# Earlier first routing, a norm between the index writes, and gated sums on GpSimd in a decoder layer

## The reference

```python
x = x + attn(_layernorm(x), ...)              # L0_attn
x = x + xattn(_layernorm(x), ctx_1024, ...)   # L0_xattn: softmax(Q K^T / sqrt(8)) V, then @ Wo + bo
x = x + ffn(_layernorm(x), ...)               # L0_ffn:

scores = jnp.einsum('bsd,de->bse', x, Wr) + br
_, topk_idx = jax.lax.top_k(scores, K)                        # K = 2 of E = 8
indicator = jax.nn.one_hot(topk_idx, E).sum(-2)
weights = jax.nn.softmax(jnp.where(indicator > 0, scores, neg_inf), axis=-1)
for i in range(E):
    xi = x * indicator[..., i:i + 1]
    h = jax.nn.relu(jnp.einsum('bsd,dh->bsh', xi, W1[i]) + b1[i])     # 128 -> 512
    yi = jnp.einsum('bsh,hd->bsd', h, W2[i]) + b2[i]                  # 512 -> 128
    out = out + yi * weights[..., i:i + 1]
```

## Time and profile before

| what | value |
|---|---|
| median of three runs | 336.9 us |
| profiled execution | 336.61 us |
| its span, first to last instruction | 334.9 us |
| mean granted TensorE clock | 0.949 |
| busy: PE, DVE, ACT, POOL | 279.0, 197.3, 184.1, 136.4 us |

### The profile page before, as it was taken

The page is one execution under the profiler, slowest core; times in us unless marked ns, Lnnn a source line. Parts: engine busy times, 40 slices in busy tenths (PEclk is TensorE's granted clock), DMA queues, the critical chain, the costliest instruction groups (busy, mean ns, idle before and its releaser), DMA issues.

```text
span 334.9 us, 5929 instructions
## 1 busy us (share of the span) xinstructions
PE 279.0 (83%) x2035; PEld 206.1 (62%) x2035; DVE 197.3 (59%) x471; ACT 184.1 (55%) x513; POOL 136.4 (41%) x188
## 2 busy tenths in 40 slices
PE   5799999999989898978996886804539989988984
PEld 2677777877866675645553343402229989988973
DVE  3768564556297866774674752521453675565564
ACT  1779767378556663654576687503314555544431
POOL 7990460317032004310387854274381346544000
PEclk9999999999999999999998999775957999999999
DMA  8800035511950100010592700010062634500302
GB/s 241 192 1 3 4 46 66 64 15 41 229 116 0 48 2 3 3 33 17 152 251 54 231 0 5 1 40 24 18 178 78 230 116 138 187 18 11 96 0 64
DMA packets 27291, 25.24 MB, mean 75 GB/s; under 512 B 3866, under 2 KB 20332, under 8 KB 27260
## 3 DMA queue, kind: packets, MB, share of 16 engines
q1 hardware_dynamic: 24462, 22.46, 25.7%
q0 software_dynamic: 1216, 1.61, 1.6%
q10 hardware_dynamic: 1584, 0.80, 0.9%
HBM read 12.49 MB, written 4.80 MB: 52 GB/s over the span
## 4 chain that ended last, share of the span: by engine, by line
PE 57%; DVE 18%; issue 9%; DMA 5%; POOL 5%; ACT 3%; SPq 3%; POOLq 0%; ACTq 0%; DVEq 0%
PE ps L873 6%; PE ps L799 5%; PE ps L800 5%; PE ps L801 5%; PE ps L906 5%; PE ps L918 4%; PE ps L951 4%; DVE mneg L1534 3%; PE ps L988 3%; PE ps L1135 3%; POOL xs L685 3%; PE ps L880 2%; SPq L478 2%; PE ps L1137 2%; DVE hid_lo L1705 2%
## 5 line engine op out<-in xcount | busy, mean ns | idle before, releaser
L1254 ACT ACTIVATE p<-ps,negmax 128x256 f32<-128x256 f32 (+1 forms) x128 | 52.7, 426 | 25.2 <-DVE negmax L1505 24.9
L1534 DVE TENSOR_REDUCE mneg<-ps 128x2 f32<-128x512 f32 x64 | 42.5, 684 | 19.7 <-PE ps L951 19.6
L1284 ACT ACTIVATE px<-ps 128x512 f32<-128x512 f32 x64 | 36.2, 599 | 19.1 <-PE ps L973 18.8
L1505 DVE TENSOR_REDUCE negmax<-ps 128x2 f32<-128x512 f32 (+1 forms) x48 | 32.9, 686 | 19.6 <-PE ps L875 12.4
L1705 DVE SCALAR_TENSOR_TENSOR hid_lo<-ps,hid_hi 128x512 fp32r<-128x512 f32 x42 | 28.6, 689 | 25.7 <-ACT hid_hi L1327 25.6
L1327 ACT ACTIVATE hid_hi<-ps 128x512 fp32r<-128x512 f32 x42 | 25.1, 598 | 33.7 <-PE ps L801 33.6
L692 POOL DMA_INDIRECT ys<-yrow,xr x26 | 25.4, 976 | 27.5 <-DVE yrow L1711 21.3
L951 PE MATMUL ps<-k_st,q_mem 128*128 128x256 bf16 x128 | 24.8, 278 | 10.1 <-DVE mneg L1534 7.6
L596 POOL TENSOR_SCALAR tmp<-mv 128x2 f32<-128x2 f32 x8 | 1.8, 230 | 68.7 <-DVE mv L1529 68.5
L1240 ACT CAST t_hi<-ps 128x512 fp32r<-128x512 f32 x32 | 18.8, 592 | 19.5 <-PE ps L801 18.5
L1254 ACT ACTIVATION_READ_ACCUMULATOR p<-ps,negmax 128x1 f32 x128 | 26.6, 208 | 0.0
(11 more groups left out here) (268 smaller groups left out, 761.1 us busy)
## 6 DMA issues: line engine op xcount, KB each, us to landing
ovw<-w_hi SPq DMA_DIRECT2D x10, 256.0 KB, 3.0
ovw<-w_lo SPq DMA_DIRECT2D x10, 256.0 KB, 3.1
w_raw<-in_L_ffn_W SPq DMA_DIRECT2D x2, 1024.0 KB, 8.1
xs<-pad SPq DMA_DIRECT2D x1, 1716.0 KB, 10.3
k_st<-k_part SPq DMA_DIRECT2D x12, 128.0 KB
q_mem<-q_part SPq DMA_DIRECT2D x48, 32.0 KB
w_last<-in_L_ffn_W SPq DMA_DIRECT2D x4, 256.0 KB, 7.3
w_late<-in_L_ffn_W SPq DMA_DIRECT2D x4, 256.0 KB, 5.2
```

The costliest lines, as they stand in the source:

```text
L1254: last = act.activation(dst, bank[:, n * i:n * i + n], ACT.Exp, bias=negmax[:, kt, h:h + 1], accum_out=psums[:, kt, h:h + 1])
L1284: act.activation(px[:, (g // 2) % 2, c0:c0 + 512], ps[:, score_banks[k], :], ACT.Exp, scale=SCALE_X).then_inc(s_px, 1)
L1505: dve.tensor_reduce(dst, ps[:, k % 3, :].rearrange("p (h q) -> p h q", h=n), AX, ALU.max, negate=True).then_inc(s_max, 1)
L1534: dve.tensor_reduce(mneg[:, qt, :].rearrange("p (r g) -> p r g", r=2)[:, :, g], ps[:, max_bank[("MX", b, u)], :].rearrange("p (h k) -> p h ...
```

## The change

Four things are changed. First, the last output product of batch 2, the router's product of group 0 and `oq0` of batch 2 stand in a slot of their own in front of the first scores of batch 3, `NT` 0 in the last slot of batch 2, and `PS` 0 in the first slot of batch 3; the rest of batch 2's output comes half a slot to a slot earlier. Second, six small VectorE instructions that prepare the places of group 1 leave `places` and become a unit `PX` behind batch 2's residual. Third, GpSimd issues three of the eight writes of group 0, then `norm_3(2)`, then the other five and those of group 1; two low parts of the second weights move behind all writes. Fourth, the gated sums leave VectorE: GpSimd does them behind its last collect, each as a product and a sum.

```diff
+FIRST_OUT = 3
...
-            for g, unit in zip(((0, 0, 1, 2, 3, 5.5, 6.5), (1.5, 2.5, 3, 4.5, 5.5), (0.5, 1.5, 2, 3, 3.5), (0.5, 1, 1.5, 2, 2.5))[b], units):
+            for g, unit in zip(((0, 0, 1, 2, 3, 5.5, 6.5), (1.5, 2.5, 3, 4.5, 5.5), (0.5, 1.5, 2, 3, 3.5), (-1, 0, 0.5, 1.5, 2))[b], units):
...
-                    (2, 7): [("W2", 0, 1)], (3, -0.5): [("NT", 0)], (3, 0): [("RT", 0), ("XC", 1)],
-                    (3, 1): [("W2", 0, 2)], (3, 2): [("PS", 0)], (3, 3): [("W2", 0, 3)], (3, 4): [("NT", 1)],
-                    (3, 5): [("RT", 1), ("XC", 2)], (3, 6): [("W2", 0, 4)], (3, 6.5): [("PS", 1)]}
+                    (2, 7): [("W2", 0, 1), ("NT", 0)], (3, 0): [("XC", 1), ("PS", 0)], (3, 1): [("W2", 0, 2)],
+                    (3, 2): [("PX", 0)], (3, 3): [("W2", 0, 3)], (3, 4): [("NT", 1)], (3, 5): [("RT", 1), ("XC", 2)],
+                    (3, 6): [("W2", 0, 4)], (3, 6.5): [("PS", 1)]}
+            if b == last:
+
+                slots.append([("CO", b - 1, 3), ("RT", 0), ("oq0", b - 1)])
...
-                if g == 0 and b >= 1:
+                if g == 0 and 1 <= b < last:
                     slot += [("CO", b - 1, 3)]
...
-                  (4, 1, "h"): [("GT", 0)], (5, 1, "h"): [("WT", 0), ("GS", 1)],
-                  (NS + 6, 0, "h"): [("CB", 0)], (NS + 6, 1, "h"): [("CB", 1)], (NS + 7, 0, "h"): [("CB", 2)]}
+                  (4, 1, "h"): [("GT", 0)], (5, 1, "h"): [("WT", 0), ("GS", 1)]}
...
+            def add_pairs(b):
+                pool.wait_ge(s_yg[b], 16)
+                pool.wait_ge(s_gate, b // 2 + 1)
+                pool.wait_ge(s_n3, TPB * (b + 1))
+                for c in range(2):
+                    for t in range(TPB * b, TPB * b + TPB):
+                        row = yg[:, 2 * t + c, :]
+                        step(pool.tensor_scalar(row, row, gate[:, 2 + c, t:t + 1], None, ALU.mult))
+                        pool.tensor_tensor(resid[:, t, :], row, resid[:, t, :], ALU.add).then_inc(s_sum, 1)
+                    pool.wait_ge(s_sum, 2 * TPB * b + TPB * (c + 1))
...
-            for i in range(4):
-                second_weights(i)
+            second_weights(0)
+            second_weights(1)
             pool.wait_ge(s_init, 16)
-            for t in range(ROUTED[0][1]):
-                for c in range(2):
-                    dispatch(t, c)
+            early = [(t, c) for t in range(*ROUTED[0]) for c in range(2)]
+            for t, c in early[:FIRST_OUT]:
+                dispatch(t, c)
             norm_3(2)
+            for t, c in early[FIRST_OUT:]:
+                dispatch(t, c)
             for t in range(*ROUTED[1]):
                 for c in range(2):
                     dispatch(t, c)
+            second_weights(2)
+            second_weights(3)
             second_weights(4)
...
             for j in range(NS):
                 collect(j)
+            for b in range(B - 1):
+                add_pairs(b)
...
-                if g == 0:
-
-                    step(dve.tensor_tensor(base[:, :], now, delta, ALU.mult))
...
+            def carry():
+
+                now, delta = over[:, 0, :], shift[:, 0, :]
+                step(dve.tensor_tensor(base[:, :], now, delta, ALU.mult))
...
-            def add_pairs(b):
-                dve.wait_ge(s_yg[b], 16)
-                dve.wait_ge(s_n3, TPB * (b + 1))
-                for c in range(2):
-                    for t in range(TPB * b, TPB * b + TPB):
-                        dve.scalar_tensor_tensor(resid[:, t, :], yg[:, 2 * t + c, :], gate[:, 2 + c, t:t + 1],
-                                                 resid[:, t, :], ALU.mult, ALU.add).then_inc(s_sum, 1)
-                    dve.wait_ge(s_sum, 2 * TPB * b + TPB * (c + 1))
...
+                    elif kind == "PX":
+                        carry()
```

More of the change, by code:

```diff
@@ L265, in decoder_layer @@
         s_ovw = [sem(f"s_ovw{i}") for i in range(2)]
-        s_b2T, s_yev = sem("s_b2T"), sem("s_yev")
+        s_b2T, s_yev, s_gate = sem("s_b2T"), sem("s_yev"), sem("s_gate")
         s_rank, s_rank_ev = sem("s_rank"), sem("s_rank_ev")
@@ L1604, in two_gates @@
                 step(dve.tensor_tensor(gate[:, 3, ts], gate[:, 1, ts], gate[:, 2, ts], ALU.mult))
+                dve.sem_inc(s_gate, 1)
             def gates():
@@ L1658, in places @@
                                   ALU.add).then_inc(s_pos, 1)
-                if g == 0:
-                    step(dve.tensor_tensor(base[:, :], now, delta, ALU.mult))
-                    step(dve.tensor_tensor(base[:, :], base[:, :], tile0[:, :], ALU.add))
-                    step(dve.tensor_scalar(edge[:, :], now, float(CAP), float(CAP), ALU.mult, ALU.add))
-                    step(dve.tensor_reduce(taken[:, :], now, AX, ALU.add))
-                    step(dve.tensor_scalar(start[:, :], taken[:, :], float(CAP), float(CAP * NE), ALU.mult, ALU.add))
-                    step(dve.tensor_tensor(full[:, :], start[:, :].to_broadcast([P, NE]), edge[:, :], ALU.subtract))
+            def carry():
+                now, delta = over[:, 0, :], shift[:, 0, :]
+                step(dve.tensor_tensor(base[:, :], now, delta, ALU.mult))
+                step(dve.tensor_tensor(base[:, :], base[:, :], tile0[:, :], ALU.add))
+                step(dve.tensor_scalar(edge[:, :], now, float(CAP), float(CAP), ALU.mult, ALU.add))
+                step(dve.tensor_reduce(taken[:, :], now, AX, ALU.add))
+                step(dve.tensor_scalar(start[:, :], taken[:, :], float(CAP), float(CAP * NE), ALU.mult, ALU.add))
+                step(dve.tensor_tensor(full[:, :], start[:, :].to_broadcast([P, NE]), edge[:, :], ALU.subtract))
             def spares():
@@ L1775, in _ @@
                         finish_rows()
-                    elif kind == "CB":
-                        add_pairs(b)
 _INS = ['x', 'ctx_1024', 'L0_attn_W_qkv', 'L0_attn_b_qkv', 'L0_attn_W_o', 'L0_attn_b_o',
```

## The result

The changed kernel takes 325.22 us, the median of four runs (323.1 to 325.4; two more, at 322.95 and 325.57, leave it where it is), against 336.97 in the same session (336.76 to 337.2). The ratio is 0.963, with a 95% interval of 0.959 to 0.968. The forecast was 325.4. Its mechanism is the one that the trace shows, though several terms had the wrong size, and these made up for each other.

What follows compares the result with a forecast made beforehand. Bound: from 216 to 250 us, group 0's places and batch 2's norm with what follows, TensorE waiting 13.6 us. Gain 11.0 + 0.8 - 0.9 + 0.8 - 0.2 = 11.5 (9.7 to 14.0), giving 325.4; range 323.0 to 329.0.

Steps and rivals of the forecast that it cites:

- Places of group 0: Routing passage: with the last `CO` of batch 2 moved ahead, these places end at 211.95 instead of 216.73, 4.8 us earlier.
- The norm of batch 2: On GpSimd, bound by VectorE's statistics: starts at 217.3 instead of 228.29, gain 11.0 us (10.6 to 11.8).
- From the norm to the places of group 1: Chain behind batch 2's norm, 8.18 us before: gains 0.8 from more full clock, between nothing and 1.5.
- The collision of `spares`: Before the first `x_lo`: VectorE's two-input additions wait for GpSimd's moved low parts, costing 0.9 us (0 to 1.6).
- starved entirely: Worst case for `spares`: VectorE's additions get nothing through beside GpSimd's low parts, costing 1.6 us.
- The end: Last `hid_lo` on VectorE: gains 0.8 us without the gated sums, which GpSimd hides by nearly 5 us.
- The 0.2 set aside: Experts' end: 0.2 us lost if one `x_lo` with two SBUF inputs meets GpSimd's sum instructions.
- the slower rival: At the end, GpSimd's sums finish last: at 1.30 us an instruction the time is 338.2; chance 0.04.
- The late statistics: Batch 2's statistics come no earlier than 220.16, so the norm starts at 220.3 and the time is 328.4; chance 0.12.
- Wider collisions: VectorE instructions with one SBUF input also wait beside GpSimd: 3.0 us worse, 328.4 to 329; chance 0.08.
- That the norm gains only what the places gain: Something else orders batch 2's norm, so only 4.8 + 0.6 is left: 331.5 us; chance 0.06.
- Two signs of being wrong: TensorE waits elsewhere over 3 us between 216 and 236, or first `x_lo` to the end changes by over 1.5 us.

Runs made afterwards that it cites:

- the repeat: The changed kernel run once more with no edit, in the first set of experiments; 323.8 us, ratio 0.961.

## Why the prediction was right

**Places of group 0.** They end at 210.83, 5.9 earlier than before, or 4.66 without the 1.24; the forecast was 4.8. Moving `CO`, `RT` and the counting did what the prediction says (with the 1.24 added, `oT0` comes at 208.40 against 208.35), and the kernel with the slots alone shows that it pays only because GpSimd is free then.

**The norm of batch 2.** The bound is the one named, statistics behind `wo`, and three writes end 1.4 before it. The size was off: 10.2 instead of 11.0, below my lower end of 10.6. The forecast laid the statistics between 216.5 and 217.5 and chose 217.3. Without the 1.24 they are at 218.0. The cause is TensorE's clock: it was 0.50 for the whole stretch from 206 to 216, so that the `CO` took 1.94 where I reckoned with at most 1.67, and `wo` 1.22 instead of 1.06. The kernel with `wo` ahead of that `CO` starts the norm 1.3 earlier, as the rows ask. There, and in an execution that was granted more clock (the one with the sums on VectorE), the third write is the bound: its end and the norm's start are 0.1 apart. That the first write came 0.86 behind the places, not 0.28, cost nothing in the profiled execution, since its cover is those 1.4.

**From the norm to the places of group 1.** Here the sum was mis-sized: "I take 0.8", at most 1.5, and it is 1.9. The mechanism, a TensorE that comes out of work and not out of 13.6 us of waiting, was right. I counted only `CO`, `NT` and `RT`, 1.5 in all, and took half of it. All of TensorE's instructions of the chain are slower at half clock, the four scores between them too: of the 1.9, `CO` gives 0.85, `NT` and `RT` 0.44 and the scores 0.6 to 0.7 (differences of start times). The executions in which TensorE waits 7 to 14 us for the norm have 8.1 to 8.4 here, those with a wait of 2 us or less 6.3, and 6.77 where there is none.

**The collision of `spares`.** -0.9 forecast, -0.9 found, and 0.9 won back when the low parts moved. How it came about was not as worked out. I let each of VectorE's additions wait for one low part, three of them by the end. In truth the first addition met the second of the four low parts and was held until the fourth had ended, 3.04 us, and the others ran freely at 0.20. That is the case that I had called starved entirely and priced at 1.6. It cost 0.9, because `spares` has 11 instructions in the trace and not 12, and the low parts ended 10.0 behind the places and not 10.2. So the size agrees by luck. The Trainium skill's rule in GPSIMD Engine Reference, Specifications (shared SBUF interfaces, contention where a VectorE instruction has two SBUF inputs) stands: `rank` with two inputs was stretched from 0.13 to 3.04.

**The end.** 0.6 forecast (0.8 less 0.2), 1.1 found. I had read 0.73 from the last `hid_lo` alone. The last `hid_hi` is late too, by 0.4, since the sum groups delay the `hid_lo` before it and with it TensorE; I had named that effect and left it at 0.1. The 0.2 set aside for an `x_lo` with two SBUF inputs wasn't lost. In the profile of after it kept its 0.69, and it was GpSimd's sum beside it, which started second, that took 0.73 instead of 0.46 (in the kernel with `wo` ahead the sum started 0.02 before the `x_lo`, and the `x_lo` took 0.98):

```profile
307.57 0.69 DVE L1723 TENSOR_TENSOR x_lo<-x_f,x_hi 128x512 fp32r<-128x512 f32 x1 [0.69 <-ACT x_hi L1342]
```

```profile
307.85 0.73 POOL L700 TENSOR_TENSOR resid<-px,resid 128x128 f32<-128x128 f32 x1
```

GpSimd's products cost 0.60 and not 0.45, the sums 0.46 as worked out from the two wider rows, and all of it 14.4 us instead of 12.2, hidden as before. The mean is 0.60 with the gaps, so the slower rival, which decides from 0.77, had the less margin for it, but the margin held.

**The rivals.** The late statistics (norm at 220.3) didn't come: 216.75, or 218.0 with the 1.24. Wider collisions didn't either, in this kernel: `hid_lo` kept 0.69. But an instruction with one SBUF input can be held: `pos_i` in the kernel with the slots alone took 0.86 instead of 0.17, until the low part beside it had ended. That the norm gains only what the places gain is refuted by both halves of the change: with the slots alone the places are early and the norm isn't, with GpSimd's order alone it is the other way round.

**The signs.** Two signs of being wrong were drawn too narrowly. TensorE does wait for over 3 us between 216 and 236: 3.88, until 235.12, for the sorted rows to be read back. It is the wait of 3.95 that ended at 248.53 before, moved forward with the chain, not a new one. And the experts' stage is 1.1 shorter in the first profile but 1.9 in the repeat, over the 1.5, since the clock at its start was higher.

**The median.** The changed kernel's profiled execution lies 2.1 below its median, so the agreement of 325.2 and 325.4 to 0.2 is luck in part. The terms as measured sum to 12.3, 0.8 above the forecast, and the repeat in the first set gives 13.0. The upper end of the range of gains should have been 14.2 by its own terms, not 14.0, which changes nothing.

The best kernel of the study is the changed one with the four low parts behind the last norm: 322.89 and, once more, 322.61 us.

## What to carry to other kernels

A gain in one chain counts only if the engine at its end is free: look at what stands in that engine's own list, and whether it waits for a third one, before an earlier input is given a value. When a wait of TensorE goes, add the instructions behind it at full clock, all of them and not only the large ones. When an effect is smaller than the spread of the runs, compare the distance in the traces between two events that have the changed instructions between them and little else, and check that the granted clock there was the same.

## What the runs showed that was not expected

- An addition of 128x8 on VectorE with two inputs in SBUF stood 3.04 us (2.42 in the repeat) from within a series of four low parts of 1.27 us that GpSimd ran back to back, and ended when the fourth did: it didn't get in between two of them. It takes 0.13 alone. GpSimd lost nothing there: its four took 4.92 us together. With GpSimd's sums it went by the order of the starts: where `x_lo` was at work first, the sum took 0.73 instead of 0.46, and where the sum was first, `x_lo` took 0.98 instead of 0.69.
- A conversion of 128x8 on VectorE with one input, both ends in SBUF (`pos_i`), took 0.86 instead of 0.17 beside a low part and ended with it, while the reduction just ahead of it, beside the same low part, kept its 0.22.
- GpSimd's product of 128x128 with one scalar for each row takes 0.60 us, where two of its norm rows of 128x127, which have two such scalars, take 0.91 together. Its sum of 128x128 takes 0.46.
- The same instructions in the same order were granted a clock of 0.50 in one execution and 0.83 in another, which moves this kernel's passage by 1.3 us. A second such place, from 176 to 188 us, has the full clock in some executions, and where it hasn't, batch 2 mostly ends 1.2 to 1.6 us later, once 2.6. A third, at the start of the experts, moves the rest by up to 1.4 us (0.77 and 0.58 in 8 us).
